# State carries as transfers of the sync engine, one diagonal row block fewer, two norm rows on GpSimd

## The reference, cut to what matters

```
x: (8, 2048, 512) f32
h = layernorm(x)
xp = h @ x_proj_w.T                       # 64 ranks, 16 B columns, 16 C columns
delta = softplus(xp[..., :64] @ dt_proj_w + dt_proj_b)          # (b, l, 512)
for each of 16 states n, for each channel d, along the 2048 steps l:
    s[l] = exp(delta[l] * A[d, n]) * s[l-1] + delta[l] * B[l, n] * h[l]
    y[l] += s[l] * C[l, n]
x = x + y + D * h
q = int8 rounding of layernorm(x), with a scale for each row
out = x + (q @ weight_q.T) * row scale * weight_scale + bias
```

## Time and profile before

| | |
|---|---|
| median of 3 runs | 2831.61 us (2831.39 to 2831.76) |
| the profiled execution, its own time | 2833.72 us |
| its span, first to last instruction | 2832.0 us |
| granted TensorE clock, mean | 0.997 |
| busy share of the span: PE, POOL, ACT, DVE | 98%, 97%, 96%, 96% |
| weight loads of PE | 89% |
| busy share of the 16 DMA engines in the middle of the run | 0.45 |

### The profile page before, as it was taken

How to read it: one execution, slowest core, us unless ns; L and a number is a source line. 1 busy time by engine, 2 the same in 40 slices (tenths; PEclk the granted TensorE clock), 3 DMA queues, 4 the chain that set the end, 5 groups by cost and what they waited for, 6 DMA issues and landing times.

```text
span 2832.0 us, 59781 instructions
## 1 busy us (share of the span) xinstructions
PE 2780.2 (98%) x22644; PEld 2515.4 (89%) x22644; DVE 2718.1 (96%) x2797; ACT 2730.5 (96%) x5086; POOL 2760.6 (97%) x1136
## 2 busy tenths in 40 slices
PE   7999999999999999999999999999999999999997
PEld 6889899899899898998998998989989989989896
DVE  6999999999999999999999999999999999999995
ACT  7999999999999999999999999999999999999993
POOL 4999999999999999999999999999999999999997
PEclk9999999999999999999999999999999999999999
DMA  5244544444435445444445454454444443544433
GB/s 188 91 107 92 133 116 114 120 105 102 131 109 124 104 94 134 116 116 118 106 102 131 109 124 105 94 133 116 114 120 105 102 131 109 124 105 110 110 94 79
DMA packets 198369, 321.23 MB, mean 113 GB/s; under 512 B 93057, under 2 KB 93057, under 8 KB 181698
## 3 DMA queue, kind: packets, MB, share of 16 engines
q1 hardware_dynamic: 164242, 250.29, 28.7%
q0 software_dynamic: 33840, 67.11, 15.5%
HBM read 212.70 MB, written 104.66 MB: 112 GB/s over the span
## 4 chain that ended last, share of the span: by engine, by line
PE 56%; POOL 26%; issue 15%; DVE 1%; DMA 1%; SPq 0%; POOLq 0%; ACT 0%; DVEq 0%
POOL A L492 20%; PE Y L724 18%; PE PB L702 13%; PE PB L699 11%; PE PM L764 3%; PE Y L720 2%; PE PM L783 2%; POOL C L509 2%; PE PM L827 2%; PE PM L812 1%; POOL C L501 1%; PE PM L792 1%; PE PM L754 1%; DVE A L853 1%; POOL XN L446 1%
## 5 line engine op out<-in xcount | busy, mean ns | idle before, releaser
L492 POOL TENSOR_TENSOR A<-A,CB 128x2048 f32<-128x2048 f32 x511 | 2349.3, 4723 | 38.0 <-DMA CB<-c_rows 27.9
L853 DVE TENSOR_TENSOR_SCAN A<-A,CAR,PB 128x512 f32<-128x512 f32 x1536 | 1844.9, 1261 | 19.2 <-PE PB L699 9.4
L548 ACT ACTIVATE A<-DEL,an 128x512 f32<-128x512 f32 x2048 | 1377.0, 719 | 1.0 <-PE Y L724 0.6
L724 PE MATMUL Y<-idf,A 128*128 128x128 f32 x8192 | 1125.7, 273 | 3.0 <-POOL A L492 3.0
L724 PEld LDWEIGHTS Y<-idf,A 128*128 128x128 f32 x8192 | 945.2, 141 | 84.2 <-issue 67.2
L569 ACT ACTIVATE DB<-XN,BC 128x512 f32<-128x512 f32 x1472 | 1003.9, 719 | 0.0
L702 PE MATMUL PB<-idf,DB 128*128 128x128 f32 x5888 | 857.3, 274 | 23.7 <-DVE A L853 20.9
L702 PEld LDWEIGHTS PB<-idf,DB 128*128 128x128 f32 x5888 | 683.5, 142 | 54.4 <-DVE A L853 39.0
L853 DVE TENSOR_TENSOR_SCAN A<-A,PB 128x512 f32<-128x512 f32 x512 | 590.9, 1203 | 24.4 <-PE PB L702 9.6
L699 PEld LDWEIGHTS PB<-DG,XN 128*128 128x128 f32 x4608 | 564.5, 192 | 43.1 <-issue 31.8
L699 PE MATMUL PB<-DG,XN 128*128 128x128 f32 x4608 | 598.9, 275 | 2.9 <-DVE A L853 2.9
(11 more groups left out here) (92 smaller groups left out, 1656.0 us busy)
## 6 DMA issues: line engine op xcount, KB each, us to landing
CB<-c_rows SPq DMA_DIRECT2D x128, 1024.0 KB, 5.9
DG<-b_diag SPq DMA_DIRECT2D x160, 256.0 KB, 5.7
out<-bib SPq DMA_DIRECT2D x32, 1024.0 KB, 8.6
out<-X POOLq DMA_DIRECT2D x32, 1024.0 KB, 9.4
X<-in_x SPq DMA_DIRECT2D x31, 1024.0 KB, 5.7
out<-C POOLq DMA_DIRECT2D x31, 1024.0 KB, 9.0
b_diag<-DG SPq DMA_DIRECT2D x2, 1280.0 KB, 12.4
b_diag<-BC SPq DMA_DIRECT2D x160, 2.0 KB, 5.1
```

The lines of the kernel that those rows point to most:

```text
L492: gp.tensor_tensor(A[s % NA][:, :, :], A[s % NA][:, :, :], CB[:, s % (4 * NG), :].unsqueeze(1).broadcast_to([128, KB, L]), ALU.mult).then_ ...
L548: act.activation(A[s % NA][:, g, :], DEL[k % 2][:, g, :], ACT.Exp, scale=an[:, g, n:n + 1])\
L724: i = pe.matmul(Y[j][:, g * 128:(g + 1) * 128], A[s % NA][:, g, j * 128:(j + 1) * 128], idf[:, :], is_transpose=True, start=False, stop=(n ...
L853: dve.tensor_tensor_scan(A[s % NA][:, g, :], A[s % NA][:, g, :], PB[(4 * s + g) % NPB][:, :], init, ALU.mult, ALU.add).then_inc(s_scan, 1)
```

## The change

The carry is no longer an ACT instruction. SP issues it as a transfer of 128x4 values, and each state has a semaphore of its own. ROWS of state 8 goes from 2 to 1: one more row block goes by act_b and a transpose. NXP goes from 3 to 2. PLACES, FIRST and LAST are all new; below, of those, the entries of which the text speaks.

```diff
-        "carry": (102, 204, 242, 307, 343, 400, 473, 529, 548, 645, 725, 771, 806, 890, 959, 1003),
+        "carry": (162, 276, 284, 301, 312, 336, 352, 422, 599, 789, 865, 1004, 1043, 1075, 1092, 1115),
-        "load": (-2254,),
-        "load_c": (182, 217, 454, 460),
-        "load_g": (-462, -101, -48, 314, 516),
+        "load": (-1872,),
+        "load_c": (76, 277, 337, 790),
+        "load_g": (-19, 1, 96, 187, 326),
-        "stats0": (-1955, -1886, -1671, -1662),
-        "store_c": (-389,),
-        "store_g": (-534,),
+        "stats0": (-1948, -1946, -1903, -1896),
+        "store_c": (-506,),
+        "store_g": (-370,),
-        "xn": (-839,),
-        "xn_p": (-818, -794, -779),
+        "xn": (-798, -771),
+        "xn_p": (-657, -600),
...
 FIRST = {
...
-        "carry": (-108, 80),
+        "carry": (-115, -4),
-        "load_c": (-91, 210, 221, 1054),
...
-    ROWS = {2: 4, 5: 4, 8: 2, 11: 4, 14: 4}
+    ROWS = {2: 4, 5: 4, 8: 1, 11: 4, 14: 4}
...
-    NXP = 3
+    NXP = 2
...
-        s_car = sem("s_car")
+        s_car = [sem(f"s_car{n}") for n in range(NS)]
...
-        def car_done(s):
-            full, k = divmod(s + 1, NS)
-            return (full - full // CPB) * NS + (k if full % CPB != CPB - 1 else 0)
+        def carried(k):
+
+            return 16 * (k + 1 - (k + 1) // CPB)
...
+            def carry(k, n):
+                s = NS * k + n
+                if k % CPB != CPB - 1:
+                    sp.wait_ge(s_scan, 4 * (s + 1))
+                    sp.dma_start(CAR[:, n, :], A[s % NA][:, :, L - 1], allow_slow_non_contiguous=True)\
+                      .then_inc(s_car[n], 16)
...
-                store_g=lambda p, i: store_g(p), load_g=load_g, put_bias=lambda p, i: put_bias(p))
+                store_g=lambda p, i: store_g(p), carry=carry, load_g=load_g, put_bias=lambda p, i: put_bias(p))
...
-                    gp.wait_ge(s_car, car_done(s))
+                    gp.wait_ge(s_car[n], carried(k))
...
-            def carry(k, n):
-                s = NS * k + n
-                if k % CPB != CPB - 1:
-                    act.wait_ge(s_scan, 4 * (s + 1))
-                    act.activation(CAR[:, n, :], A[s % NA][:, :, L - 1], ACT.Copy).then_inc(s_car, 1)
...
-                        dve.wait_ge(s_car, car_done(s - NS))
+                        dve.wait_ge(s_car[n], carried(k - 1))
```

More of the change, by code:

```diff
@@ L70 @@
-        "xn_p": (-818, -794, -779),
-        "xp_out": (-475,),
-        "xt_out": (-705, -658, -626, -603),
+        "act_b": (-148, -121, -116, -115, -102, -65, -62, -7, 3, 8, 9, 59, 101, 102, 119, 150, 154, 168, 234,
+        239, 259, 263, 265, 336, 373, 403, 420, 426, 486, 490, 516, 523, 565, 583, 586, 609, 621, 650, 662,
+        673, 675, 692, 702, 772, 786, 812, 820),
+        "add_c": (2204,),
+        "add_x": (1659,),
+        "aggr0": (-1290,),
+        "amax": (1420,),
+        "ascale": (1555,),
@@ new lines @@
+        "q_t": (1906, 1928, 1975, 2005),
+        "qt_out": (1903, 1925, 1938, 2007),
+        "root": (1490,),
+        "rstd0": (-885,),
+        "scale_a": (2094, 2133, 2153, 2174),
+        "scale_out": (3225, 3280, 3617, 3889),
+        "scale_p": (1988, 2071, 2080, 2190),
+        "scales": (1619,),
+        "scan": (-43, -38, -25, -12, 41, 42, 47, 54, 64, 123, 147, 176, 197, 240, 256, 267, 273, 284, 286,
+        291, 293, 294, 294, 380, 386, 394, 417, 421, 422, 427, 480, 493, 515, 522, 528, 549, 550, 565, 578,
@@ new lines @@
+        600, 603, 653, 679, 681, 683, 691, 724, 725, 786, 787, 787, 787, 793, 834, 838, 881, 890, 901, 908,
+        909, 917, 926, 928, 949),
+        "shift0": (-801,),
+        "square": (1346, 1349, 1370, 1400),
+        "stats0": (-1948, -1946, -1903, -1896),
+        "step": (1575,),
+        "store_c": (-506,),
+        "store_g": (-370,),
[8 rows of a table added]
+        "times_c": (-32, 214, 410, 457, 464, 502, 515, 531, 572, 586, 592, 601, 695, 703, 706, 729),
+        "var1": (1528,),
+        "weights": (-104,),
@@ L82 @@
[L82 to L85, removed]
-        "load_c": (-91, 210, 221, 1054),
[L87 to L103, removed]
+        "act_b": (-295, -287, -277, -252, -219, -206, -194, -189, -102, 37, 41, 92),
+        "aggr0": (-1876,),
+        "b_c": (-1325,),
@@ new lines @@
+        "bc_out": (-678,),
+        "carry": (-115, -4),
+        "d_t": (-1547, -1461, -1285, -738),
+        "decay": (-314, -269, -181, -181, -174, -104, -94, -83, 33, 54, 69, 124),
+        "delta": (-1059, -927, -921, -834),
+        "dl_t": (-616, -595, -557, -404),
+        "du": (-731, -596, -366, -191),
+        "load": (-1733,),
+        "load_g": (-290, -126, 255, 260, 629),
+        "log0": (-2895,),
+        "rstd0": (-2512,),
+        "scan": (-133, -104, -99, -68, -65, -59, -31, 23),
@@ new lines @@
+        "shift0": (-2474,),
+        "stats0": (-2751, -2641, -2261, -2165),
+        "store_c": (-1229,),
+        "store_g": (-780,),
+        "tb": (-370, -329, -288, -253, -245, -200, -142, -132),
+        "th": (192, 198, 200, 249),
+        "times_c": (-392, -32),
+        "x_p": (-1831, -1677, -1671, -1645),
+        "x_t": (-2468, -2245, -2199, -2168),
+        "xn": (-2163, -1922),
+        "xn_p": (-2018, -1196),
+        "xp_out": (-1288,),
+        "xt_out": (-1824, -1801, -1412, -1330),
@@ L120 @@
[L120 to L126, removed]
+        "act_b": (-148, -121, -116, -115, -102, -65, -62, -7, 3, 8, 9, 59, 101, 102, 119, 150, 154, 168, 234,
+        239, 259, 263, 265, 336, 373, 403, 420, 426, 486, 490, 516, 523, 565, 583, 586, 609, 621, 650, 655,
+        662, 662, 662, 662, 664, 731, 731, 736),
@@ new lines @@
+        "add_c": (4094,),
+        "add_x": (1818,),
+        "amax": (3668,),
+        "ascale": (2555,),
+        "centre": (3887, 4290, 4587, 4896),
+        "decay": (-98, -94, -93, -85, -71, -71, -65, -43, -5, 73, 79, 84, 128, 134, 138, 163, 172, 180, 185,
+        189, 197, 198, 201, 228, 235, 241, 274, 280, 289, 365, 393, 401, 406, 412, 425, 432, 438, 449, 451,
+        456, 478, 509, 530, 531, 533, 533, 534, 536, 728, 733, 737, 746, 746, 746, 766, 766, 774, 774, 812,
+        816, 835, 837, 847, 849),
@@ new lines @@
+        "gather": (1158, 1256, 1447, 1776),
+        "idle": (3624, 3653, 3669, 3862),
+        "inv": (3689,),
+        "last_q": (4206, 4248, 4341, 4677),
+        "put_bias": (2436,),
+        "q_mm": (4319, 4565, 5149, 5585),
+        "q_t": (4127, 4208, 4426, 4660),
+        "qt_out": (4013, 4049, 4216, 4418),
+        "root": (3507,),
+        "scale_a": (5496, 6005, 6354, 6386),
+        "scale_out": (6910, 7141, 7563, 7726),
+        "scale_p": (4535, 4704, 4706, 4718),
+        "scales": (3770,),
@@ new lines @@
+        "scan": (-43, -38, -25, -12, 41, 42, 47, 54, 64, 123, 147, 176, 197, 240, 256, 267, 273, 284, 286,
+        291, 293, 294, 294, 380, 386, 394, 417, 421, 422, 427, 480, 493, 515, 522, 528, 549, 550, 565, 578,
+        600, 603, 653, 679, 681, 683, 691, 724, 725, 786, 787, 787, 787, 818, 818, 818, 821, 832, 832, 834,
+        834, 834, 835, 843, 843),
+        "square": (1210, 1477, 1677, 1761),
+        "step": (3952,),
[8 rows of a table added]
+        "times_c": (-32, 214, 410, 457, 464, 502, 515, 531, 572, 586, 592, 601, 675, 743, 876, 983),
@@ L674, in _ @@
                 xp_out=lambda p, i: xp_out(p), bc_out=lambda p, i: bc_out(p),
-                qt_out=qt_out, scale_a=scale_a, decay=decay, act_b=act_b,
-                carry=carry)
+                qt_out=qt_out, scale_a=scale_a, decay=decay, act_b=act_b)
         @block.tensor
```

88 lines of the change are left out of this document (23 added, 65 removed), and 24 rows, old and new, of tables (LAST, PLACES).

## The result

The changed kernel takes **2869.16 us** (median of 4 runs, 2867.05 to 2872.44) against 2831.50 for the kernel before (4 runs, 2831.12 to 2831.76): a ratio of 1.0135 with a 95% interval of 1.0123 to 1.0147, slower by some 38 us. The forecast was 2816 with a range of 2805 to 2840, so both the sign and the range were wrong.

The account below looks back on a forecast made before the run. POOL was taken as the bound. From the profiled 2833.7 us: -22.8 for the norm row over 31 chunks, +6 returned by other engines, +1 start, giving 2817.9; the median of runs is 2.1 lower: 2816 us, range 2805 to 2840.

Parts of the forecast that it names:

- What bounds the kernel: Whole chunk, kernel before: POOL's instruction sum is the period, 86.5 to 86.6 us; PE is close behind.
- One norm row leaves POOL: On POOL, two L446 instructions fewer, 0.735 us a chunk: from 86.6 to 85.9 us.
- ACT: ACT's chunk: carries leave, 1.32 us arrives; 85.4 us with carries, 85.3 without; the 0.4 waited ahead of carries goes.
- another engine takes over: PE, DVE or ACT waits grow as POOL is freed; period stays 86.3 to 86.6, time 2825 to 2836; chance 0.20.
- State 8 on PE: On PE, eight records leave and four transposes come: -0.45 us a chunk, from 86.1 to about 85.65.
- The carries on SP: Carries as SP transfers, 12 a chunk: landing in 3 to 4 us, ends 2.5 and 11; no mid-run cost.
- The rival had the price (2871): Late-carry rival: POOL waits before L492 in 24 carrying chunks; 2.6 us uncovered costs 62, returns 23: 2871; chance 0.15.
- What the Trainium skill says against this part: Carry transfers: strided elements and small transfers are mostly overhead; a lone carry estimated at 2 us, the sum unchanged.
- What stands behind SP's waits: SP's in-order queue: carries behind load_c and store_g are held only briefly; no cost, margins 3 to 4 us.
- the load of X: Issued two chunks ahead instead of three; DVE wants X after 9.4 us, landing takes 5.7; no cost.
- the DMA share: The 16 DMA engines: 12 carries a chunk raise the share from 0.45 to at most 0.60, costed at nothing.
- The start: First chunk: C's first load behind carries 0 and 1 starts POOL 6.5 us later, mostly caught up; +1 us.

Follow-up runs that it names:

- the two runs on theory D: Kernel before, each with one change: one norm row moved from POOL to ACT, 2845.51 us; state 8 cut to one diagonal row block, 2840.80 us.
- the early add_x: Changed kernel with add_x, the output's adding transfer of X, issued ahead of unit 2 instead of unit 12, and put_bias moved earlier: 2850.15 us, ratio 1.0062.

## Why the prediction was wrong

*What bounds the kernel.* "So POOL is the bound" was half right. The prediction's own numbers for ACT in a carrying chunk were 85.7 busy, 0.4 waited for scans and 0.4 for transposes: 86.5 of 86.6. ACT was nearly as full as POOL in those chunks, and I read its busy share alone as 0.9 us of room; the two runs on theory D give 0.3. 0.70 us more on it cost 12.7 us.

*One norm row leaves POOL*: right. The forecast was 85.9 us of work and waits; with the carries in time POOL's busy union is 85.6.

*ACT*: the second step that failed. "85.4 and 85.3" measured 85.74 with the early add_x, and the waits of 0.4 that were to "go too" came back as DB<-XN, 17.8 us in 29 chunks. ACT's sum is 86.7, above POOL's 86.35 of before. Of the 0.735 that POOL gave up, the forecast let 0.2 return. The early add_x, almost without late carries, has a period of 86.84 against 86.54: all 0.735 returned, and 0.3 on top. The rival "another engine takes over" had the right event, but stopped at 86.6, as it reckoned that the others would at most stay where they were.

*State 8 on PE*: the worth was wrong, and the price on PE isn't seen. PE's union is 86.1 us with one row block and 86.00 with two (early add_x, state 8 at 1 and at 2), against 86.16 before: the 0.45 us did not come off it. ACT pays 0.8 us for it (85.74 against 84.93) where 0.62 was forecast, and didn't have them.

*The carries on SP*: the first step that failed, and the largest. "I cost the delay at nothing in the middle" took a landing of 3 to 4 us, with 11 as the end for a carry right behind a load of C, and looked for the least lead in the kernel before, at unit 0. The landing is 2.0 us, and 7.5 to 8.3 beside GpSimd's adding transfer; the place is unit 13 or 14. The prediction followed what SP has queued ahead of a carry, and not what POOL's own queue has in flight: out<-X, 9.4 us to land, was a row of the page of before, and its move stood in the diff. The rival had the price (2871) by luck. It took 2.6 us uncovered at unit 0 in 24 chunks, 62 us, and let 23 us of the change's gain stand against them. Measured were 63.7 us in 39 waits at another place, of which taking away 51 us brought only 21 us of time, since ACT then fills the period; and ACT leaves nothing of the gain.

*What the Trainium skill says against this part*: "The trace agrees that 2 KB land no sooner than 1 MB does" was misread, as 5.1 us are sooner than 5.9, and the 5.1 are of five transfers at once. The fit of 2.0 us plus bytes, which the Trainium skill gives for the path of GpSimd's transfers, came out for a lone carry on SP's (2.0 us). "The sum stays the same" did not hold beside other transfers. The profile's pages count 401121 packets in the changed kernel against 198369, which is 528 more for each of 384 carries, and a carry has 512 values. Whether 2 KB in fewer packets would pass sooner, no run here shows.

*What stands behind SP's waits, the load of X, the DMA share*: right. DVE waited 10.6 us for X, in 4 waits of the whole run; the share went from 0.45 to at most 0.48 in the four chunks.

*The start*: "I take +1, ends 0 and 6.5". The first unit begins at 46.69 instead of 41.77, 4.9 us later, and none of it is caught up; the cure is worth 7.7. What failed is that "most of it is caught up": the waits for carries in the first chunks were taken as slack, and they are longer in the changed kernel (13.5 us against 9.5).

*The sum by its causes*, from the ratios to the kernel before (0.0001 is 0.28 us): late carries 1.0135 to 1.0062, 20.7 us; the row block of state 8 1.0062 to 1.0008, 15.3 us; the first load of C 1.0008 to 0.9980, 7.9 us. What is left of the change is then 5.7 us faster than before, where 15.5 were forecast. The intervals of these ratios are 0.0009 to 0.0017 wide to either side, 3 to 5 us, and each term is read with the repairs before it in place.

## What to carry to other kernels

A synchronization that passes through a DMA is priced by what else is in flight when it is issued, on the other engines' queues too, and not by its median: here it landed when the large transfer ahead of it did. List the large transfers, the adding ones first, against the few instructions that have least lead. An in-order engine's load is its busy time plus the waits that recur in each round; when that sum is within a few tenths of the period (here 86.5 of 86.6 us) it is a bound, however its share stands to another's. And when two engines share the bound, only work that leaves both is worth moving.

## What the runs showed of the hardware

A transfer of 128x4 single values from SBUF to SBUF takes SP 0.60 us to issue and lands in 2.0 us in the median (lowest 1.9). The Trainium skill, DMA: Bandwidth & Descriptors, section Anatomy of one DMA, gives about 2.0 us as the fixed cost of a transfer on the path that GpSimd's transfers take; this one goes by SP's, and the trace has the same number. The strided last dimension added nothing to see to a transfer that was alone.

Landing of the same transfer by what was in flight: behind a plain 1 MB load of SP's own queue 3.5 us (carry at 1260.96, X's load at 1258.72); behind a plain 1 MB write of GpSimd's queue 5.2; behind an adding transfer of GpSimd's queue 5.9 (out<-C at 1277.81), 7.5 and 8.3. In each of these cases, and in the 7.3 us of the run with C's load moved, the carry lands 0.1 to 0.2 us after the large transfer ahead of it. Adding makes the transfer itself longer, 9.2 against 5.9 us in the median, and its issue on POOL, 1.25 against 0.86; a carry behind it lands later by as much (8.3 against 5.2 us).

The same page of the Trainium skill, section Queues, rings and completion order, says that each engine goes round the queues with work and drains a packet from each. By that a carry on SP's queue would pass GpSimd's 1 MB in turns. The changed kernel's trace shows no even turns: of the carry issued at 1157.48 no packet moves before 1160, where in the next chunk all 528 of an undisturbed one have moved within 2.1 us of the issue; from 1160 to 1164 SP's queue moves 190 packets of single values beside 391 of the adding transfer, and the rest follow as that runs out. Why SP's queue has to wait so long, no run here tells.
